# Decoder layer on one core: the softmax's division inside the probability splits, a unit's split in its own step, and a reordered start of the quantised product

## What is computed

```python
x = x + attn(layernorm(x), Wq, Wk_down, Wv_down, Wk_up, Wv_up, Wo)
x = x + fake_quant(layernorm(x)) @ fake_quant(ctx_4096)
x = x + ffn(layernorm(x), A_w, B_w, Wq_w, keys)

# attn: 32 query heads of 128, 8 key-value heads from latents of 32 each
scores = einsum('bhqd,bhkd->bhqk', q, k) / sqrt(128)
attn = softmax(where(causal, scores, -1e9))
out = einsum('bhqk,bhkd->bhqd', attn, v) ... @ Wo.T
# fake_quant(x) = (clip(round(x / s + z), 0, 255) - z) * s
# ffn: z = x @ A_w.T (64 experts x 8), gated by the softmax of the 16 best
#      of 64 router scores, times B_w.T, times 2
```

## Time and profile before

| | |
|---|---|
| median of 3 runs | 1134.34 us (1133.69 to 1134.78) |
| the profiled execution | 1134.8 us |
| its span in the profile | 1133.0 us |
| PE busy | 1077.2 us, 95% |
| DVE busy | 907.1 us, 80% |
| ACT busy | 536.7 us, 47% |
| POOL busy | 411.0 us, 36% |
| mean granted clock of PE | 0.991 |

### The profile page before, as it was taken

One profiled execution on the slowest core, in us unless ns is written; L12 is line 12 of the kernel. 1 busy time (PEld: TensorE's weight loads), 2 busy tenths in 40 slices (PEclk: granted clock), 3 DMA queues, 4 the chain that ended last, 5 costly groups with the idle time before them and its releaser, 6 DMA issues.

```text
span 1133.0 us, 19870 instructions
## 1 busy us (share of the span) xinstructions
PE 1077.2 (95%) x6361; PEld 580.2 (51%) x6368; DVE 907.1 (80%) x1868; ACT 536.7 (47%) x1094; POOL 411.0 (36%) x423
## 2 busy tenths in 40 slices
PE   4999988999999999999999999999999999799997
PEld 3876544455545554555555455545554544345553
DVE  6789588978787878788888878787978897888853
ACT  4656366544444545454445545454545462343421
POOL 2049655534343435334343534343534242000000
PEclk8999999999999999999999999999999999999999
DMA  7026147544454445445545544444545578000001
GB/s 300 1 82 236 75 93 155 139 109 118 125 132 105 100 122 147 111 121 129 114 102 135 136 111 104 120 120 111 128 123 114 124 180 267 1 1 38 35 23 56
DMA packets 200865, 128.66 MB, mean 114 GB/s; under 512 B 171376, under 2 KB 173552, under 8 KB 199920
## 3 DMA queue, kind: packets, MB, share of 16 engines
q1 hardware_dynamic: 200816, 128.03, 43.4%
HBM read 68.23 MB, written 17.83 MB: 76 GB/s over the span
## 4 chain that ended last, share of the span: by engine, by line
PE 78%; DVE 10%; DMA 3%; ACT 3%; issue 3%; SPq 1%; POOL 0%; DVEq 0%; ACTq 0%; POOLq 0%
PE ps L1535 73%; DMA k_t<-kv_parts 3%; PE ps L1785 3%; DVE prob L1297 2%; ACT prob L968 1%; DVE wo_sb L1091 1%; DVE h_b L1091 1%; DVE prob_s L1091 1%; SPq L526 1%; DVE stats L1099 1%; PE ps L1801 1%; PE ps L1853 1%; DVE prob_t L1091 1%; DMA o_t<-in_wdown 1%; PE ps L1549 0%
## 5 line engine op out<-in xcount | busy, mean ns | idle before, releaser
L705 POOL TENSOR_SCALAR prob<-prob,row_inv 128x128 f32<-128x128 f32 (+3 forms) x256 | 203.4, 813 | 450.5 <-DVE row_inv L1268 450.5
L1535 PE MATMUL ps<-wo_sb,o_t 128*128 128x512 f16 x1536 | 351.2, 380 | 3.7 <-DVE x_sb L1279 3.6
L1535 PE MATMUL ps<-h_b,wq_sb 128*128 128x512 f16 x1524 | 340.9, 380 | 0.0
L968 ACT ACTIVATE prob<-prob,neg_max 128x128 f32<-128x128 f32 (+3 forms) x256 | 140.6, 550 | 234.1 <-DVE neg_max L1303 234.1
L1535 PEld LDWEIGHTS ps<-h_b,wq_sb 128*128 128x128 f16 x1524 | 148.3, 98 | 177.4 <-issue 0.3
L1535 PEld LDWEIGHTS ps<-wo_sb,o_t 128*128 128x128 f16 x1536 | 147.2, 98 | 172.4 <-DVE x_sb L1279 6.9
L1279 DVE SCALAR_TENSOR_TENSOR x_sb<-ps,x_sb 128x512 f32<-128x512 f32 x256 | 174.2, 686 | 54.9 <-PE ps L1535 53.9
L1535 PE MATMUL ps<-k_t,q_t 128*128 128x512 f16 (+3 forms) x768 | 115.3, 301 | 10.6 <-DMA k_t<-kv_parts 9.3
L1535 PE MATMUL ps<-prob_t,v_sb 128*128 128x128 f16 (+2 forms) x960 | 118.0, 277 | 6.3 <-DMA prob_t<-prob_s 6.3
L1297 DVE CUSTOM_DVE_ANT_0 prob<-ps,mask 128x512 f32<-128x512 f32 (+3 forms) x256 | 110.3, 485 | 2.3 <-issue 1.6
L1255 DVE SCALAR_TENSOR_TENSOR q_tmp<-ps,q_tmp 128x512 f32<-128x512 f32 x105 | 72.1, 687 | 40.4 <-PE ps L1535 38.4
(11 more groups left out here) (141 smaller groups left out, 1172.9 us busy)
## 6 DMA issues: line engine op xcount, KB each, us to landing
wq_in<-in_wq SPq DMA_DIRECT2D x64, 256.0 KB, 3.4
wo_in<-in_wo SPq DMA_DIRECT2D x32, 512.0 KB, 3.9
side_in<-in_ctx SPq DMA_DIRECT2D x16, 512.0 KB, 4.4
kv_parts<-wo_sb SPq DMA_DIRECT2D x7, 1024.0 KB, 5.3
x_sb<-in_x SPq DMA_DIRECT2D x8, 512.0 KB, 9.3
ctx_quantised<-side_out SPq DMA_DIRECT2D x16, 256.0 KB, 2.9
h_b<-ctx_quantised SPq DMA_DIRECT2D x2, 2048.0 KB, 11.2
out<-x_sb SPq DMA_DIRECT2D x8, 512.0 KB, 2.6
```

Source lines behind the costliest of these rows:

```text
L705: ins = nc.gpsimd.tensor_scalar(at, at, row_inv[:, u % 2, q:q + 1], S_P, ALU.mult, ALU.mult)
L968: ins = nc.scalar.activation(at, at, ACT.Exp, bias=neg_max[:, n % 2, q:q + 1], scale=SOFTMAX, accum_out=row_sum[:, n % 2, q:q + 1])
L1535: ins = nc.tensor.matmul(out_, lhs(i), rhs(j), start=start and n == 0, stop=stop and n == 3 * len(pairs) - 1)
```

## The change

It does eight things, all in the order or the form of work:

1. POOL's four multiplications per unit go. DVE multiplies the four reciprocals of a unit by 2^8 (one 128 x 4 instruction behind the reciprocal, which it waits for). The high split on ACT and the low split on DVE become four instructions each, one per query tile, with the reciprocal as an operand per partition.
2. The split of unit u stands in step u, behind the output split (ACT) and behind the second addition (DVE); before, it stood in step u + 1, ahead of the exponentials (ACT) and right behind the maxima (DVE).
3. SP loads the next head's keys in unit 7 ahead of the transposes of unit 6.
4. Wup is loaded into three buffers instead of two.
5. The first eight of the last chunks use banks 6 and 7 alone; the column sums use banks 3 and 4, stand among these chunks, and their scaled form lies where Wq's blocks were.
6. x of tile 0 is turned four chunks before the end of the last sixteen, and the quantised products of tile 0 and tile 1 follow each other at once, tile 1's in banks 5 and 7.
7. For each tile, the two halves of the last product stand apart, the h3 transposes between them; the turn of the gated z comes behind the second half, but ahead of it for the last tile. DVE's additions follow that order.
8. On ACT the sums of x's rows come later in a tile's step.

```diff
-COLUMN_BANK = (X_BANK, (Z_BANK, ZT_BANK))
+COLUMN_BANK = (3, 4)
+SECOND_X_BANK = (Z_BANK, ZT_BANK)
+
+
+def x_banks(t):
+
+    return SECOND_X_BANK if t == 1 else X_BANK
...
-        up_in = turned[:, 0:2048].bitcast(F32).rearrange("p (n d) -> p n d", n=2)
-        up = turned[:, 2048:4096].rearrange("p (n m d) -> p n m d", n=2, m=2)
+        up_in = turned[:, 0:3072].bitcast(F32).rearrange("p (n d) -> p n d", n=3)
+        up = turned[:, 3072:5120].rearrange("p (n m d) -> p n m d", n=2, m=2)
...
+                        if u == 7 and not last:
+                            load_k(g + 1)
                         turn(g, u - 1)
...
-                    pool.wait_ge(inv_done, UNITS * g + u + 1)
-                    pool.sem_inc(pool_passed)
-                    for q in range(QT):
-                        at = prob[:, u % 2, S_AT[q]:S_AT[q] + (q + 1) * P]
-                        ins = nc.gpsimd.tensor_scalar(at, at, row_inv[:, u % 2, q:q + 1], S_P, ALU.mult, ALU.mult)
-                    ins.then_inc(prob_normed, 1)
...
-                act.wait_ge(prob_normed, UNITS * g + n + 1)
+                act.wait_ge(inv_done, UNITS * g + n + 1)
                 if not (isinstance(g, int) and g == 0 and n == 0):
 
                     act.wait_ge(p_turned[(n - 1) % 2], 32 * (UNITS // 2 * g + (n - 1) // 2 + 1))
-                split_hi(prob_s[:, 0, :], prob[:, n % 2, :], p_hi, 1.0)
+                for q in range(QT):
+                    at = slice(S_AT[q], S_AT[q] + (q + 1) * P)
+                    ins = nc.scalar.activation(prob_s[:, 0, at], prob[:, n % 2, at], ACT.Copy, scale=row_inv[:, n % 2, q:q + 1])
+                ins.then_inc(p_hi, 1)
...
-                    if not (first and u == 0):
-                        p_split(g, u - 1)
                     exponentials(g, u)
                     if not (first and u < LAG):
                         o_split(g, u - LAG)
+                    p_split(g, u)
...
-                nc.vector.reciprocal(row_inv[:, n % 2, :], row_sum[:, n % 2, :]).then_inc(inv_done, 1)
+                nc.vector.reciprocal(row_inv[:, n % 2, :], row_sum[:, n % 2, :]).then_inc(inverted, 1)
+                dve.wait_ge(inverted, UNITS * g + n + 1)
+                nc.vector.tensor_scalar(row_inv[:, n % 2, :], row_inv[:, n % 2, :], S_P, None, ALU.mult).then_inc(inv_done, 1)
...
-                split_lo(prob_s[:, 1, :], prob[:, n % 2, :], prob_s[:, 0, :], p_lo, 1.0)
+                for q in range(QT):
+                    at = slice(S_AT[q], S_AT[q] + (q + 1) * P)
+                    ins = nc.vector.scalar_tensor_tensor(prob_s[:, 1, at], prob[:, n % 2, at], row_inv[:, n % 2, q:q + 1],
+                                                         prob_s[:, 0, at], ALU.mult, ALU.subtract)
+                ins.then_inc(p_lo, 1)
...
-                    if not (first and u == 0):
-                        p_split(g, u - 1)
                     step_add(g, u, 0)
                     inverses(g, u)
                     if not (first and u < LAG):
                         o_split(g, u - LAG)
                     step_add(g, u, 1)
+                    p_split(g, u)
...
-                    if i == 2:
-                        p_split(g, UNITS - 1)
                     pair0_add(i)
+                column_add(0)
                 wo_split(g, 3)
                 o_split(g, UNITS - 2)
                 for i in range(WO_STEP, 2 * WO_STEP):
                     pair0_add(i)
+                    if i == WO_STEP + 1:
+                        column_add(1)
                 o_split(g, UNITS - 1)
...
             for i in range(WO_STEP):
                 pair0_chunk(i)
+            column_sums(0)
             outputs(KV_HEADS - 1, UNITS - 2)
             for i in range(WO_STEP, 2 * WO_STEP):
                 pair0_chunk(i)
+                if i == WO_STEP:
+                    column_sums(1)
             outputs(KV_HEADS - 1, UNITS - 1)
             for c in range(WO_CHUNKS):
                 pair1_chunk(c)
-
-            def column_sums(b):
-                pe.wait_ge(ctx_summed, KT * (b + 1) + 1)
-                for j in range(2):
-                    nc.tensor.matmul(ps[:, COLUMN_BANK[b][j], :], ones[:, :], ctx_sum[:, b, j * HALF:(j + 1) * HALF],
-                                     start=True, stop=True).then_inc(column_done, 1)
-
-            for i in range(-1, TT + STEPS_AHEAD):
-                if i == 0:
-                    pe.wait_ge(wo_read, max(last_reader(bank) for bank in X_BANK))
-                    column_sums(0)
-                if 0 <= i < TT:
-                    t, b = i, i // QT
-
-                    pe.wait_ge(x_qt_copied, t + 1)
-                    if t == 0:
-                        pe.wait_ge(wo_read, LAST_WO + 2 * WO_STEP + WO_CHUNKS)
-                    if t == 0:
-                        pe.wait_ge(column_read, 2)
-                    if t % QT == 0:
-                        pe.wait_ge(ctx_loaded[b], 16)
-                    for j in range(2):
-                        if t >= 3:
-                            pe.wait_ge(out_done, 2 * (t - 3) + j + 1)
-                        for k in range(KT):
-                            ins = nc.tensor.matmul(ps[:, X_BANK[j], :], x_qt[:, t % 2, k * P:(k + 1) * P],
-                                                   ctx_q[:, b, k, j * HALF:(j + 1) * HALF], start=k == 0, stop=k == KT - 1)
-                    ins.then_inc(x_done, 1)
-                    if t == 0:
-                        column_sums(1)
+                if c == WO_CHUNKS - 4:
+                    turn_x(0)
+            turn_x(1)
+            x_product(0)
+            x_product(1)
...
+                if i == TT:
+                    turn_z(TT - 1)
+                if 0 <= i - 2 < TT:
+                    out_product(i - 2, 1)
+                if 0 <= i - 1 < TT - 1:
+                    turn_z(i - 1)
```

More of the change, by code:

```diff
@@ L164 @@
 LAST_WO = wo_number(KV_HEADS - 1, UNITS, 0) - 1
-PAIR0_BANK = (6, 7, 3, 4)
 PAIR1_BANK = (0, 1, 2, PV_BANK, 6, 7, 3, 4)
@@ L302, in decoder_layer @@
         wo_loaded = [sem(f"wo_loaded{n}") for n in range(2)]
-        up_loaded = [sem(f"up_loaded{n}") for n in range(2)]
+        up_loaded = [sem(f"up_loaded{n}") for n in range(3)]
         stored = sem("stored")
@@ L415, in _ @@
                 sp.dma_start(x_sb[:, t, :], x[t]).then_inc(x_loaded[t], 16)
-            for n in range(2):
+            for n in range(3):
                 sp.dma_start(up_in[:, n, :], wup[KV_ORDER[n]]).then_inc(up_loaded[n], 16)
@@ L562, in group @@
                         load_ctx(0)
-                    if u == 7 and not last:
-                        load_k(g + 1)
             load_chunk(0, 0)
             for n in range(KV_HEADS - 1):
-                if n + 2 < KV_HEADS:
+                if n + 3 < KV_HEADS:
                     sp.wait_ge(up_lo, n + 1)
-                    sp.dma_start(up_in[:, n % 2, :], wup[KV_ORDER[n + 2]]).then_inc(up_loaded[n % 2], 16)
+                    sp.dma_start(up_in[:, n % 3, :], wup[KV_ORDER[n + 3]]).then_inc(up_loaded[n % 3], 16)
                 if n == 4:
@@ L1038, in _, with copy_turned @@
                 scale_rows(t)
+            def copy_turned(t):
+                act.wait_ge(x_turned, t + 1)
+                nc.scalar.activation(x_qt[:, t % 2, :], ps[:, TURN_BANK, :].bitcast(BF16), ACT.Copy).then_inc(x_qt_copied, 1)
+            copy_turned(0)
             sum_rows(0)
-            for i in range(-1, TT + STEPS_AHEAD):
-                if 0 <= i and i + 1 < TT:
-                    sum_rows(i + 1)
+            copy_turned(1)
+            sum_rows(1)
+            for i in range(0, TT + STEPS_AHEAD):
                 if 0 <= i - 1 < TT:
@@ L1066, in _ @@
                         .then_inc(weighted, 1)
+                if 1 <= i and i + 1 < TT:
+                    sum_rows(i + 1)
                 if 0 <= i < TT - STEPS_AHEAD:
@@ L1362, in pair0_add, with column_add @@
             def pair0_add(i):
-                wo_add(LAST_WO + i + 1, PAIR0_BANK[i % 4], 2 * WO_STEP + i)
+                wo_add(LAST_WO + i + 1, WO_BANK[i % 2], 2 * WO_STEP + i)
+            def column_add(b):
+                for j in range(2):
+                    dve.wait_ge(column_done, 2 * b + j + 1)
+                    nc.vector.tensor_scalar(column_term[:, b, j * HALF:(j + 1) * HALF], ps[:, COLUMN_BANK[j], :],
+                                            shift_scaled[:, 0:1], shift_scaled[:, 2:3], ALU.mult, ALU.add)\
+                        .then_inc(column_read, 1)
             def last_outputs():
@@ L1790, in _ @@
+            for i in range(TT + STEPS_AHEAD):
+                if 2 <= i < TT:
+                    x_product(i)
                 if 0 <= i - 1 < TT:
```

143 lines of the change are left out of this document (78 added, 65 removed).

## The result

| | before | changed |
|---|---|---|
| median | 1133.69 us (1131.15 to 1134.78, 5 runs) | 1223.53 us (1222.99 to 1225.06, 5 runs) |
| profiled execution, span | 1133.0 us | 1221.9 us |
| PE busy / idle | 1077.2 / 55.8 us | 1101.8 / 120.1 us |

The changed kernel takes 1.0795 times as long [1.0779, 1.0811]. The forecast of 1194 us had the side right and its range (1150 to 1224) just holds the time, but the size is 30 us short. That the range holds it is luck: its upper end was priced for a lower clock and longer delays, and the time got there by a cost that the forecast did not have. Its sign for PE came half: PE is idle 64.3 us longer (forecast: some 60), but its busy time, forecast as unchanged, is 24.6 us longer for the same 6361 instructions, at a mean granted clock of 0.978 instead of 0.991.

The account below looks back on a forecast made before the run. PE bounds the kernel before (104.0 of 105.42 us in a steady head), and the change makes DVE the bound. Terms +37.7, +16.3, +9.7, +3.0, -5.2, -1.4, -0.5 sum to +59.6 on 1134.8: about 1194 us, range 1150 to 1224.

Parts of the forecast that it names:

- sign for PE: PE over the whole run: busy time unchanged, idle time up by some 60 us, in waits for DVE's x_sb, q_tmp and wq_sb.
- six steady heads: DVE's list of 107.0 us plus 4.65 of delays beside POOL makes 111.7 a head against 105.42: +37.7 us over six.
- first head: First key-value head: DVE binds sooner, its list takes 98.7 us against 82.4 before: +16.3 us.
- last head, units 0 to 3: First four units of the last head: left at zero.
- last head, units 4 to 7: Last four units of the last head: DVE sets the pace, 47.0 us against 37.26: +9.7 us.
- last chunks, column sums: Behind the last head: column sums add 3.0 us of DVE and 0.9 of PE, last probability split (1.4) goes: +3 us.
- transition to the third product: Last chunk to third quantised product: with x of tile 1 ahead, 26.2 us instead of 31.4: -5.2 us.
- third product to the end, Wup: Last stage: earlier turn of z hides a 1.4 us wait (-1.4); third Wup buffer lets its load start earlier (-0.5).
- The step of a unit on DVE: DVE, each unit: block splits begin 8.55 us after the maxima instead of 5.96, with dearer pieces and a wait for ACT.
- rival 2: DVE's delays beside POOL grow to some 7.5 us a head, with a lower clock in the first head: 1218 us; chance 0.15.
- Rival 1: DVE is the bound, but the delays fall into its waits: 107.0 us a head, 1166 us; chance 0.2.
- rival 3: Faster: four pieces cost what one did, DVE's list falls under 104.0 us, PE binds everywhere: 1112 us; chance 0.1.

Follow-up runs that it names:

- written out: The changed kernel with DVE's six steady heads as straight code instead of a loop; 1207.8 us, ratio 1.0658 to the kernel before.
- narrow_pool: The changed kernel with POOL's sums of Wq, clipping and context sums cut to 8 columns, output not the reference's; 1202.1 us, ratio 1.0595.
- next_step: The changed kernel with the probability splits back in the step after their own on ACT and DVE; 1127.4 us, ratio 0.9946.
- pieces_only: The kernel before plus the earlier key load and the division inside the splits, without the splits' move or the reordered ending; 1124.4 us, ratio 0.9922.
- longer_loop: The kernel before with 32 semaphore increments that nobody waits for added to DVE's loop body; 1134.3 us, ratio 1.0010.
- shift by 96: The changed kernel with 96 semaphore increments that nobody waits for at the start of DVE's program; 1226.9 us, ratio 1.0827.

## Why the prediction was right on the side and short in size

The steps of its sum, against the two profiled executions. The first and the steady heads are cut at the scaled maximum of unit 0. The last three cuts are the forecast's own: units 4 to 7 from the maxima of unit 4 to the end of DVE's list for unit 7 (903.94 to 941.20 before, 976.92 to 1023.76 changed), the end of the last chunk (975.10 and 1061.37) and the third quantised product (1006.51 and 1091.48).

| step | forecast | measured |
|---|---|---|
| six steady heads | +37.7 | +51.8 |
| first head | +16.3 | +19.3 |
| last head, units 0 to 3 | 0 | +1.7 |
| last head, units 4 to 7 | +9.7 | +9.6 |
| last chunks, column sums | +3.0 | +3.7 |
| transition to the third product | -5.2 | -1.3 |
| third product to the end, Wup | -1.4, -0.5 | +3.9, +0.2 |
| sum | +59.6 | +88.9 |

**The step of a unit on DVE** was right in each part: 8.59 us for 8.55. ACT's pieces and DVE's cost, by width over the run (busy us, mean ns):

```profile
L963 ACT ACTIVATE prob_s<-prob,row_inv 128x512 f16<-128x512 f32 x64 | 45.2, 706 | 0.0
L963 ACT ACTIVATE prob_s<-prob,row_inv 128x128 f16<-128x128 f32 x64 | 25.7, 401 | 2.4 <-DVE row_inv L1277 0.9
L1319 DVE SCALAR_TENSOR_TENSOR prob_s<-prob,row_inv,prob_s 128x512 f16<-128x512 f32 x64 | 47.6, 744 | 0.0
L1319 DVE SCALAR_TENSOR_TENSOR prob_s<-prob,row_inv,prob_s 128x128 f16<-128x128 f32 x64 | 22.5, 351 | 46.0 <-ACT prob_s L963 46.0
```

ACT's are the 0.40 to 0.71 us taken from the exponentials, and DVE's widest is 744 ns where the form with an operand per partition had 746.

**Steady heads** is the step that failed most, and by a missing term. The list was given as 107.0 us (107.7 without POOL), the delays as 4.65 (3.6 in the first of the six, 4.4 to 4.7 in the others), the head as 111.7 (111.95, and 111.5 written out). That the delays keep their size is partly luck: the forecast took them row by row from the kernel before, and the changed kernel has other rows. The rows of 0.4 us are gone (Wo splits and a rounding), two q_t splits lose 1.4 us each instead of 1.6 and 1.4, a third up to 1.1 in two of the heads, and the scaled maximum, which was not in the list, is held up 0.85 us once or twice a head. What the term lacked are DVE's stops at the jump back, 12.8 us. They follow from 32 instructions more in the loop body, which the forecast counted for their time on DVE and not as code.

The Trainium skill ("Runtime: NRT & Kernel Launch", Instruction fetch mechanics) says that a taken branch whose target lies outside the resident pages of instructions waits for a DMA to fetch it. The trace agrees that a jump back can wait for such a transfer: 21 packets on the instruction queue without stops, 46 with them, 2.1 to 3.6 us each stop in the changed kernel. Which instructions were resident at a jump no run shows. The prediction did not weigh that rule.

**First head.** Here too the step of a unit was right and the delays beside POOL were missing: the forecast added them to the steady heads alone. The list of 98.7 us, 3.5 us of delays (in q_t's splits and one scaled maximum) and a wait of 0.7 us for ACT make 102.9, and 102.88 were measured (against 83.6 before by this cut and 82.4 by the forecast's). DVE's waits in this head, in total, times, longest:

```profile
DVE row_inv L1275 <- ACT prob L971: 17.7, 8, 2.4
DVE prob_s L1319 <- ACT prob_s L963: 10.0, 8, 2.0
DVE q_t L1098 <- ACT q_t L741: 0.7, 1, 0.7
```

None of them is for PE. The 1.5 us a time that were kept for the upper end did come on PE (its clock was granted at 0.93 there, and after a wait of 3.67 us its 24 products took 7.03 us instead of 5.34), but DVE did not wait for them. In narrow_pool, without delays, the first head takes 100.7 us.

**Last head and last chunks.** Units 0 to 3 were left at zero and cost 1.7 us, 1.6 of them between the scaled maximum of unit 3 and the maxima of unit 4. Units 4 to 7 came as forecast. In the last chunks, after the wait at their start the clock is granted at its lower level for part of PE's next 24 products, and from there on PE is unbroken, so this counts. Before, then changed:

```profile
940.74 5.36 PE L1535 MATMUL ps<-wo_sb,o_t 128*128 128x512 f16 x24 [2.41 <-DVE x_sb L1279]
```

```profile
1023.30 7.74 PE L1548 MATMUL ps<-wo_sb,o_t 128*128 128x512 f16 x24 [4.54 <-DVE x_sb L1288]
```

That is 2.4 of the 3.7 us, and the column sums' four products are 0.9. The forecast had that 0.9 and no clock; for the 3.0 us that it gave to DVE's part of the column sums PE did not wait. In next_step, without a late DVE, the stretch from the scaled maximum of unit 7 to the last chunk's end still takes 2.7 us more than before (45.3 for 42.6): 1.7 at the lower clock, 0.9 for the column sums.

**Transition.** Its waits were forecast well: 6.8 us to the normalised tile (6.8) and 3.1 for its split (3.2). What the list lacked is the clock, 0.79 in that stage. These three rows were priced at 1.1, 1.07 and 5.35 us:

```profile
1072.29 1.76 PE L1885 MATMUL ps<-ident,k_t 128*128 128x128 f32 x8 [3.40 <-ACT k_t L1060]
1077.26 1.89 PE L1848 MATMUL ps<-wq_sb,router_sb 128*32 128x128 f16 x16 [3.21 <-DVE wq_sb L1098]
1079.08 7.17 PE L1548 MATMUL ps<-h_b,wq_sb 128*128 128x512 f16 x24
```

They and the turn behind them cost 3.8 us more, which is the missing gain. In next_step the transition wins 2.1.

**End.** The 1.4 us that the earlier turn of z was to hide are still there, a wait of 1.44 us for q_t in the last tile; what went is another, of 1.14 us, before the last router product. And four tiles wait 1.06 us, since DVE's addition comes behind a wait for ACT's tile and the addition of the column terms:

```profile
1106.75 0.69 DVE L1445 TENSOR_SCALAR prob<-prob 128x1024 f32<-128x1024 f32 x1 [0.72 <-ACT prob L1028]
...
1108.09 1.28 DVE L1465 SCALAR_TENSOR_TENSOR x_sb<-wq_in,row_term,x_sb 128x1024 f32<-128x1024 f32 x1
1109.29 0.75 DVE L1471 SCALAR_TENSOR_TENSOR x_sb<-ps,gate_scale,x_sb 128x512 f32<-128x512 f32 x1
```

```profile
1110.39 3.45 PE L1799 MATMUL ps<-h_b,q_t 128*128 128x512 bf16 x15 [1.06 <-DVE x_sb L1471]
1212.67 0.39 PE L1548 MATMUL ps<-h_b,q_t 128*128 128x512 f16 x1 [1.44 <-DVE q_t L1098]
```

The forecast read the moved lines there for what they hide, and not for what stands behind them.

**The rivals.** The time lies near rival 2's 1218, but not for its reason: the delays beside POOL did not grow. Rival 1 (delays fall into waits) is refuted by narrow_pool, since the delays counted. What rival 3 foresaw for the change happens in next_step and pieces_only: with the splits one step later the list stays under PE's 104 us and the kernel is faster than before, by 0.5 and 0.8%. The moved key load alone gives 1.0%, so this is no gain of the division inside the splits.

What stays open: the length from which DVE's body is fetched anew. It lies within the 32 instructions between the two kernels' bodies. Why the packet started later against DVE's work in narrow_pool, where a stop grew to 3.8 us on average, was not tried.

## What to carry to other kernels

An instruction whose input is a step old can fill an in-order engine's wait for free; the same instruction, moved to where its input is just being made, adds its own time, the wait it used to fill, and a new one, and here that was 96 us for a move of two calls, the stops included. Count added instructions of a loop body as code too: here a body that is fetched anew cost some 2.5 us at each jump back, hidden only while another engine was the bound. When a large edit has many parts, time each alone: here one moved DMA issue won 10.8 us, and the rest together lost what it won and 90 us more.

## What the runs showed that was not expected

- A stop of 2.1 to 3.6 us with ready inputs at a loop's jump back (1.5 to 2.1 in longer_loop, up to 4.4 in narrow_pool), named "issue" in the profile, which came with 32 more instructions in the body, of either kind tried (work or idle increments), and did not go with a shift by 96.
- A DVE instruction of 4 columns with one SBUF input is held up beside POOL too, nine times in the steady heads of the changed kernel and never in narrow_pool. In this row the scaled maximum took 1.02 us instead of 0.17 and ended at 552.89, POOL's sum beside it at 552.86. DVE's timeline, then POOL's:

```profile
551.87 1.02 DVE L1312 TENSOR_SCALAR neg_max<-row_max 128x4 f32<-128x4 f32 x1
```

```profile
551.59 1.27 POOL L662 TENSOR_TENSOR wq_in<-wq_in 128x512 f32<-128x512 f32 x1 [0.27 <-POOL q_tmp L656]
```
